# Residual input copied to the output in DRAM, results added there by accumulating DMAs, in a routed mixture-of-experts kernel

## The reference

```
xt   = x @ W.T + b + (x @ A[slot]) @ B[slot] * 2
gate = two experts of 16 for each token, with their scores
y    = sum over e of gate[:, e] * ((silu(xt @ w1[e] + b1[e]) * (xt @ w2[e] + b2[e])) @ w3[e] + b3[e])
z    = (silu(xt @ sw1 + sb1) * (xt @ sw2 + sb2)) @ sw3 + sb3
out  = x + y + z
```

## Time and profile before

| | |
|---|---|
| time, median of 3 runs | 166.63 us (165.42 to 168.01) |
| time of the profiled execution | 166.47 us |
| its span | 164.7 us |
| TensorE busy | 149.6 us (91%) |
| VectorE busy | 99.8 us (61%) |
| ScalarE busy | 52.9 us (32%) |
| GpSimd busy | 50.6 us (31%) |
| first gather issued | 72.51 us |
| first matmul of the tail | 145.53 us |
| last VectorE instruction starts | 161.57 us |
| TensorE clock granted | 1.000 over the whole span |

### The profile page before, as it was taken

The page is one execution under the profiler, slowest core; times in us unless marked ns, Lnnn a source line. Parts: engine busy times, 40 slices in busy tenths (PEclk is TensorE's granted clock), DMA queues, the critical chain, the costliest instruction groups (busy, mean ns, idle before and its releaser), DMA issues.

```text
span 164.7 us, 2590 instructions
## 1 busy us (share of the span) xinstructions
PE 149.6 (91%) x748; PEld 114.2 (69%) x749; DVE 99.8 (61%) x252; ACT 52.9 (32%) x110; POOL 50.6 (31%) x66
## 2 busy tenths in 40 slices
PE   3999999999979999997989989999999567789991
PEld 3777687887867777885867767778678355458770
DVE  2673495378967679978517873443453324358993
ACT  4542242623722161154363324324334122300000
POOL 6820240000000020436204675656656615230000
PEclk9999999999999999999999999999999999999999
DMA  5899938999965599998301467778777992336965
GB/s 170 291 359 333 412 153 247 398 423 416 400 204 211 158 374 391 384 452 284 117 13 44 153 180 228 225 271 246 222 273 236 323 401 91 115 127 223 352 256 194
DMA packets 16509, 42.62 MB, mean 259 GB/s; under 512 B 2192, under 2 KB 2192, under 8 KB 16240
## 3 DMA queue, kind: packets, MB, share of 16 engines
q1 hardware_dynamic: 11392, 25.41, 43.3%
q0 software_dynamic: 3616, 12.06, 21.7%
q10 hardware_dynamic: 1488, 4.98, 7.9%
HBM read 33.53 MB, written 8.91 MB: 258 GB/s over the span
## 4 chain that ended last, share of the span: by engine, by line
PE 69%; DVE 11%; DMA 11%; issue 4%; ACT 2%; POOL 1%; DVEq 0%; SPq 0%
PE bank L961 29%; PE bank L1133 16%; DMA xg_sb<-xt_rows,slot_tok 8%; PE bank L1151 7%; PE bank L1123 5%; DVE x_sb L911 3%; DVE x_sb L924 3%; PE bank L1021 2%; DMA xT_raw<-in_xT 2%; PE bank L1001 2%; DVE x_sb L919 2%; PE bank L1011 2%; PE bank L1032 1%; PE bank L1144 1%; PE bank L1113 1%
## 5 line engine op out<-in xcount | busy, mean ns | idle before, releaser
L1133 PE MATMUL bank<-w_sb,xgT_sb 128*128 x144 | 37.0, 382 | 1.5 <-issue 1.5
L1133 PEld LDWEIGHTS bank<-w_sb,xgT_sb 128*128 128x128 f32 x144 | 25.6, 190 | 12.5 <-issue 9.9
L451 POOL DMA_INDIRECT y_rows<-y_sb,slot_row x18 | 18.6, 1034 | 28.3 <-DVE y_sb L868 28.3
L856 DVE TENSOR_TENSOR pre_sb<-bank,b_sb 128x256 f32<-128x256 f32 x18 | 7.6, 425 | 28.2 <-PE bank L1133 21.8
L445 POOL DMA_INDIRECT xg_sb<-xt_rows,slot_tok x20 | 19.4, 971 | 11.9 <-issue 5.5
L1151 PE MATMUL bank<-w_sb,hT_sb 128*128 x36 | 18.6, 597 | 0.5 <-ACT hT_sb L594 0.5
L1123 PE MATMUL bank<-ident,xg_sb 128*128 128x128 f32 x72 | 10.9, 274 | 3.9 <-DMA xg_sb<-xt_rows,slot_tok 3.9
L961 PE MATMUL bank<-condW_h,xT_h 128*128 128x512 f32 x32 | 14.1, 441 | 0.3 <-DVE xT_l L662 0.3
L586 ACT COPY xgT_sb<-bank 128x512 f32<-128x512 f32 x18 | 10.5, 585 | 10.3 <-PE bank L1123 6.2
L961 PE MATMUL bank<-xtT_h,sw_h 128*128 128x512 f32 x32 | 13.2, 413 | 0.0
L868 DVE COPY y_sb<-bank 128x512 f32<-128x512 f32 x18 | 12.3, 684 | 1.5 <-PE bank L1151 1.5
(11 more groups left out here) (177 smaller groups left out, 277.2 us busy)
## 6 DMA issues: line engine op xcount, KB each, us to landing
w_sb<-in_w SPq DMA_DIRECT2D x8, 1024.0 KB, 9.3
w_sb<-in_w ACTq DMA_DIRECT2D x2, 2048.0 KB, 15.5
xt_rows<-xt_ring SPq DMA_DIRECT2D x8, 256.0 KB, 4.0
b_sb<-in_b SPq DMA_DIRECT2D x1, 2048.0 KB
x_sb<-in_x SPq DMA_DIRECT2D x8, 256.0 KB
low_sb<-y_rows SPq DMA_DIRECT2D x4, 512.0 KB
high_sb<-y_rows SPq DMA_DIRECT2D x4, 512.0 KB, 5.3
out<-x_sb SPq DMA_DIRECT2D x8, 256.0 KB, 2.7
```

The costliest lines, as they stand in the source:

```text
L451: pool.indirect_dma_start(y_rows, bass.IndirectOffsetOnAxis(ap=slot_row[:, b:b + 1], axis=0), y_sb[:, b % 2, :], None).then_inc(y_scattere ...
L856: dve.tensor_tensor(pre_sb[:, s % 2, :], bank[2 + s % 2][:, 0:2 * INTER], b12_sb[:, bass.ds(e * (2 * INTER), 2 * INTER)], ALU.add).then_in ...
L1133: mm = pe.matmul(bank[2 + s % 2][:, 0:2 * INTER], xgT_sb[:, s % 2, k, :], w12_sb[:, bass.ds(e * W12 + k * 2 * INTER, 2 * INTER)], start=(k ...
```

## The change

- SP no longer loads `x` into SBUF. It copies each tile of `x` to the same rows of `out`, DRAM to DRAM, at the same points of `y_copied`.
- The tiles are finished in `acc` (the place of `x_sb`). `add_low(i)` writes `low * val + shared`, `add_high(i)` adds `high * val`: two VectorE instructions per tile, in place of three for tiles 0 to 4 and two for tiles 5 to 7. The diagonal matmuls go.
- GpSimd adds each finished tile to `out` in DRAM by a DMA with `accum_op=ALU.add`; SP's stores go.
- `y_sb` becomes a ring of four (`y_place`). The waits for scatters count four semaphores, and eight registers hold the counts; VectorE's short instructions that compute them are fewer (11 go, 6 come).
- Gathers run six blocks ahead of the scatters instead of four (`AHEAD`). The ring `xg_sb` stays at four, so that a gather still waits for the transposes of the block four before it.
- TensorE loads `top` after block 0 and `left` after block 1, in place of after block 3 and after the loop, and no longer loads `first`. VectorE and ScalarE load `left` earlier too, VectorE also `first`.
- VectorE's part of the shared matrices is spread over blocks 0 to 6, which are written out up to 7.
- Of the last hidden product of the shared expert, three of four steps instead of two come before `turn_xg(0)`.

```diff
-LOW_ON_PE = (5, 6, 7)
 UNROLL = 4
+AHEAD = UNROLL + 2
+Y_RING = UNROLL
...
-        x_sb = at(112, "x_sb", [P, TILES, DIM])
+        acc = at(112, "acc", [P, TILES, DIM])
...
-        y_sb = at(132, "y_sb", [P, 2, DIM])
+        y_ring = at(132, "y_ring01", [P, 2, DIM]), at(176, "y_ring23", [P, 2, DIM])
...
+        def stored(eng, at, least):
+            return [eng.value_load(eid[0:1, at + s:at + s + 1], min_val=16 * least // Y_RING,
+                                   max_val=16 * -(-BLOCKS // Y_RING)) for s in range(Y_RING)]
...
-        def drained(eng, drain):
-
-            left = blocks_left(eng)
+        def drained(eng, left, drain):
+
...
-            sp.wait_ge(sh_up_done, 2 * IC)
             for i in range(TILES):
                 sp.wait_ge(y_copied, UNROLL + i)
-                sp.dma_start(x_sb[:, i, :], x[i * P:(i + 1) * P, :]).then_inc(x_in, 16)
+                sp.dma_start(out[i * P:(i + 1) * P, :], x[i * P:(i + 1) * P, :]).then_inc(x_in, 16)
...
+            low_counts = stored(sp, LOW_STORED_AT, LOW_BLOCKS)
+            counts = stored(sp, STORED_AT, FULL)
+            for s in range(Y_RING):
+                sp.wait_ge(y_scattered[s], low_counts[s])
+                sp.sem_inc(low_stored, 1)
+            sp.wait_ge(low_stored, Y_RING)
...
-            for n in range(TILES):
-                sp.wait_ge(acc_done, n + 1)
-                sp.dma_start(out[n * P:(n + 1) * P, :], x_sb[:, n, :]).then_inc(out_stored, 16)
             sp.wait_ge(out_stored, 16 * TILES)
...
             def group(g):
                 for b in range(g * UNROLL, (g + 1) * UNROLL):
-                    gather(b + UNROLL)
+                    if b + AHEAD < BPAD:
+                        gather(b + AHEAD)
                     scatter(b)
 
-            for b in range(UNROLL):
+            for b in range(AHEAD):
                 gather(b)
...
+            pool.wait_ge(x_in, 16 * TILES)
+            for i in range(TILES):
+                pool.wait_ge(acc_done, i + 1)
+                pool.dma_start(out[i * P:(i + 1) * P, :], acc[:, i, :], accum_op=ALU.add).then_inc(out_stored, 16)
...
-            for n, i in enumerate(LOW_ON_PE):
-                act.activation(diag[:, n, :], ident[:], ACT.Copy, scale=val[:, 0, i:i + 1]).then_inc(diag_ready, 1)
...
+            def add_low(i):
                 dve.wait_ge(shared_done, i + 1)
+                dve.scalar_tensor_tensor(out=acc[:, i, :], in0=low_tiles(first, i), scalar=val[:, 0, i:i + 1],
+                                         in1=shared_bank(i)[:], op0=ALU.mult, op1=ALU.add).then_inc(acc_shared, 1)
...
+            def add_high(i):
                 dve.wait_ge(high_in[i // 2], 16)
+                dve.wait_ge(acc_shared, i + 1)
+                dve.scalar_tensor_tensor(out=acc[:, i, :], in0=high_sb[:, i, :], scalar=val[:, 1, i:i + 1],
+                                         in1=acc[:, i, :], op0=ALU.mult, op1=ALU.add).then_inc(acc_done, 1)
+
             dve.wait_ge(low_in, 16 * TILES // 2)
+            for i in range(TILES):
+                add_low(i)
+                if i >= 3:
+                    add_high(i - 3)
+            for i in range(TILES - 3, TILES):
+                add_high(i)
...
-            shared_up(3, (1,), 0, KC // 2)
+            shared_up(3, (1,), 0, KC - 1)
...
             turn_xg(0, 0)
-            shared_up(3, (1,), KC // 2, KC)
+            shared_up(3, (1,), KC - 1, KC)
...
             for b in range(UNROLL):
                 steps(b, b)
-            top = last_group(pe)
+                if b == 0:
+                    top = last_group(pe)
+                if b == 1:
+                    left = blocks_left(pe)
...
-            first = low_at(pe)
...
-                if i in LOW_ON_PE:
-                    n = LOW_ON_PE.index(i)
-                    pe.wait_ge(diag_ready, n + 1)
-                    pe.wait_ge(low_in, 16 * TILES // 2)
-                    mm = pe.matmul(shared_bank(i)[:], diag[:, n, :], low_tiles(first, i), start=False, stop=True)
```

More of the change, by code:

```diff
@@ L45 @@
 DRAINED = BLOCKS - LOOP_END
-LOOP_AT, LEFT_AT, EVEN_AT, ODD_AT, LOW_EVEN_AT, LOW_ODD_AT, LOW_AT = range(BPAD, BPAD + 7)
+Y_RING = UNROLL
+LOOP_AT, LEFT_AT, LOW_AT = range(BPAD, BPAD + 3)
+STORED_AT, LOW_STORED_AT = BPAD + 4, BPAD + 4 + Y_RING
 LOW_BLOCKS = (K * T - T) // P
@@ L242, in program @@
         h_turned, hT_copied, y_done, y_copied = sem("h_turned"), sem("hT_copied"), sem("y_done"), sem("y_copied")
-        y_scattered = [sem(f"y_scattered{s}") for s in range(2)]
+        y_scattered = [sem(f"y_scattered{s}") for s in range(Y_RING)]
         shared_done, acc_shared = sem("shared_done"), sem("acc_shared")
-        diag_ready = sem("diag_ready")
         low_in = sem("low_in")
@@ L368, in _ @@
                              ).then_inc(low_in, 16)
[L369 to L373, removed]
+            for s in range(Y_RING):
+                sp.wait_ge(y_scattered[s], counts[s])
+                sp.sem_inc(rows_stored, 1)
+            sp.wait_ge(rows_stored, Y_RING)
             for n in range(TILES // 2):
                 sp.dma_start(high_sb[:, 2 * n:2 * n + 2], by_tile[1][:, 2 * n:2 * n + 2]).then_inc(high_in[n], 16)
-            for n in range(TILES):
-                sp.wait_ge(acc_done, n + 1)
-                sp.dma_start(out[n * P:(n + 1) * P, :], x_sb[:, n, :]).then_inc(out_stored, 16)
             sp.wait_ge(out_stored, 16 * TILES)
@@ L610, in _ @@
             top = last_group(act)
+            left = blocks_left(act)
             def group(b):
@@ L624, in _ @@
             each_group(act, 0, top, group)
-            drained(act, drain)
-            for n, i in enumerate(LOW_ON_PE):
-                act.activation(diag[:, n, :], ident[:], ACT.Copy, scale=val[:, 0, i:i + 1]).then_inc(diag_ready, 1)
+            drained(act, left, drain)
         @block.vector
@@ L828, in _ @@
             then(dve.tensor_tensor(slot_row[:], slot_f32, slot_empty, ALU.add))
[L830 to L835, removed]
+            dve.engine_nop().then_inc(slot_row_ready, 1)
+            then(dve.tensor_scalar(slots_back[:], cols[0:1, 0:Y_RING], -1.0, float(Y_RING - 1), ALU.mult, ALU.add))
+            then(dve.tensor_scalar(nused_f[:], ends[0:1, E - 1:E], 1.0 / P, None, ALU.mult))
             then(dve.tensor_scalar(low_base[:], padded[0:1, :], 0, None, ALU.is_gt))
@@ L864, in copy_y @@
                 dve.wait_ge(y_done, b + 1)
-                if not (isinstance(b, int) and b < 2):
-                    dve.wait_ge(y_scattered[s % 2], (b - s % 2) * 8)
-                dve.tensor_copy(y_sb[:, s % 2, :], bank[5 + s % 2][:]).then_inc(y_copied, 1)
+                if not (isinstance(b, int) and b < Y_RING):
+                    dve.wait_ge(y_scattered[s % Y_RING], (b - s % Y_RING) * (16 // Y_RING))
+                dve.tensor_copy(y_place(s), bank[5 + s % 2][:]).then_inc(y_copied, 1)
@@ L870, in _, with rest_hs @@
             add_bias(0, 0)
             times_up(0, 0)
[L872 to L878, removed]
+            def rest_hs(u):
+                dve.wait_ge(hs_hi, u + 1)
+                n, c = u // IC, u % IC
                 unit = (slice(None), c, slice(n * HALF, (n + 1) * HALF))
                 rest(hsT_split[1][unit], hsT_sb[unit], hsT_split[0][unit], hs_done)
[L881 to L887, removed]
@@ L888, in _, with rest_sw3, rest_b3s @@
-            top = last_group(dve)
+            def rest_sw3(c):
+                dve.wait_ge(sw3_hi, 1)
+                rest(sw3_split[1][:, c, :], sw3_raw[:, c, :], sw3_split[0][:, c, :], sw3_done)
+            def rest_b3s():
+                dve.wait_ge(b3s_hi, 1)
+                dve.tensor_tensor(b3s_split[32:64, :], b3s_raw[32:64, :], b3s_split[32:64, :].bitcast(F32), ALU.subtract
+                                  ).then_inc(b3s_done, 1)
+            for b in range(2 * UNROLL):
+                s = b % UNROLL
+                add_bias(b + 1, s + 1)
+                times_up(b + 1, s + 1)
+                copy_y(b, s)
+                if b < 4:
+                    rest_hs(b)
+                elif b < 6:
+                    rest_sw3(b - 4)
+                elif b == 6:
+                    rest_b3s()
+                if b == 4:
+                    top = last_group(dve)
+                if b == 5:
+                    left = blocks_left(dve)
+                if b == 6:
+                    first = low_at(dve)
@@ L901, in drain @@
                     copy_y(top + (UNROLL + s), s)
[L903 to L909, removed]
+            each_group(dve, 2 * UNROLL, top, group)
+            drained(dve, left, drain)
+            def add_low(i):
                 dve.wait_ge(shared_done, i + 1)
[L911 to L922, removed]
-                dve.wait_ge(high_in[i // 2], 16)
[L924 to L929, removed]
@@ L931, in _ @@
-            first = low_at(dve)
-            dve.wait_ge(low_in, 16 * TILES // 2)
[L933 to L949, removed]
@@ L1198, in _ @@
             each_group(pe, UNROLL, top, group)
-            drained(pe, drain)
```

(1 more changed line is left out.)

47 lines of the change are left out of this document (15 added, 32 removed).

## The result

| | before | after |
|---|---|---|
| time, median | 167.32 us (165.42 to 170.61, 4 runs) | 169.06 us (168.56 to 169.72, 4 runs) |
| profiled execution, time and span | 166.47 and 164.7 us | 168.87 and 167.1 us |
| start of the tail (first shared matmul) | 145.53 | 140.19 |
| end of VectorE | 162.26 | 157.0 |

The changed kernel takes 1.0174 of the time of the kernel before, 95% interval 1.0106 to 1.0242: slower, by 1 to 2.4%, where 165.2 us and a range of 162.0 to 168.6 were forecast. Some executions of a kernel are slower as a whole; the medians and ranges here hold them, the ratios leave them out. The table shows where the time went. The tail starts 5.3 us earlier and VectorE ends 5.3 us earlier, and yet the span is 2.4 us longer. All of the loss lies behind VectorE's last instruction.

A forecast was written before the change was run, and what follows sets the result against it. TensorE carries 69% of the chain, so its stalls and the tail count. Tail start 145.53 - 0.7 - 3.05 - 1.1 = 140.7, plus 22.7 of tail is 163.4 of span, plus 1.77 outside: 165.2 us, range 162.0 to 168.6.

The forecast's parts named there:

- part 6: Tail's end: GpSimd's accumulating stores finish at +22.7 us after the tail's start, making the tail 3.5 us longer.
- Part 1: Start of the blocks: three matmuls moved ahead of TensorE's 0.85 us wait for the first gather gain 0.7 us.
- Part 2: In the blocks: gathers issued earlier remove TensorE's stall for the gather of block 16, gain 3.05 us.
- The ring of four: Blocks, rows to scatter: four places in `y_sb` were said to remove no wait seen in the trace.
- Part 3: TensorE's register loads at loop entry, loop exit and ahead of the tail: gain 1.1 us, bounds 0 to 2.15.
- Part 4: Copies of x from DRAM to DRAM: cost 0, up to 3 us if they press on gathers.
- Part 5: VectorE in the tail: sixteen additions instead of 21 gain nothing, the last ending 17.15 us after the tail's start.
- Part 6, pitch 1.26: GpSimd's last four stores follow one another at 1.26 us, as its indirect DMAs do; bounds 0.33 and 1.26.
- Rival B: Tail's stores: a plain DMA costs GpSimd only 0.33 us, last issue at +17.45, time 163.6 us; chance 0.23.
- Part 6, the read, 0.9: Tail's stores: reading `out` before the addition writes it adds 0.9 us to the landing; bounds 0 and 3.6.
- The way of a plain one: Tail's stores: 2.8 us from a DMA's issue to its landing without the read, taken from the last scatter.
- rival D: Tail's accumulating DMAs don't overlap, each reading and writing back before the next; 173.6 us at 2.8 us each; chance 0.10.

The follow-up runs named there:

- e1: Changed kernel with plain stores by GpSimd in place of the accumulating ones, input left out of the sum: 164.34 us, 0.9843 of the kernel before.
- e2: Changed kernel with plain stores of `acc` by SP in place of GpSimd's accumulating ones, input left out of the sum: 161.58 us, 0.9685 of the kernel before.
- e4: Kernel before with one edit, gathers six blocks ahead: 165.87 us, 0.9949 of the kernel before.
- e6: e3 with TensorE loading `top` after block 3 and `left` after the loop, as before: 163.74 us, 0.9842 of the kernel before.
- e3: Changed kernel with the old tail (x in SBUF, old additions, diagonal matmuls, stores by SP): 161.89 us, 0.9709 of the kernel before.
- e8: Changed kernel with plain stores by GpSimd for tiles 0 to 6, accumulating for tile 7 alone, input left out of tiles 0 to 6: one run of 164.70 us.
- e10: e2 with tile 7 stored by GpSimd instead of SP, plain, input left out of the sum: one run of 163.78 us.
- e5: Kernel before with the new tail alone (x copied to `out` in DRAM, sixteen additions, accumulating DMAs by GpSimd): 174.21 us, 1.0487 of the kernel before.
- e9: Changed kernel, but tiles 4 to 7 with x in SBUF, three additions each and stores by SP: 164.06 us, 0.9854 of the kernel before.

## Why the prediction was wrong

The head and VectorE's tail went as forecast; the step that failed is part 6, "The stores by GpSimd": its 3.7 us from the last issue to the landing, of which 0.9 for the addition in DRAM, and its end of the program at that landing. The runs show 7.4 us, of which 4.6 for the addition (e1), and 2.0 more for GpSimd's drain (e2). Forecast and measured, as a sum of the span: 163.4; -0.5 for a tail that starts at 140.2 instead of 140.7; -1.9 for the last issue, at +17.1 instead of +18.97 after the tail's start; +3.7 for its landing, 7.4 us instead of 3.7; +2.4 for the time from that landing to the end, which the forecast had at nothing. That gives 167.1, the span measured. Of the 2.4, 0.4 lie behind the last landing in the kernel before too; the prediction took the span's end, 164.7, for that landing, which was at 164.3.

- **Part 1, 0.7:** 0.66 (the wait of 0.85 is now 0.19). Right.
- **Part 2, 3.05:** the stall is gone, so the size is right. But its reason was half of the truth. "The ring of four takes away no wait that the trace shows" was true and misleading: that wait was hidden behind the other one, and e4 uncovered it. Without the ring, which the forecast priced at nothing, the early gathers bring the tail forward by 2.3 us instead of 3.05, and are worth 1.1 us of span.
- **Part 3, 1.1:** the three gaps of 2.15 us became 0.41, a gain of 1.7, within the bounds. e6 puts 1.0 us on the two moved loads; e3 shows 0.54 for a tail that loads `first`.
- **Part 4, 0:** right. The copies DRAM to DRAM held nothing up, and e2, which has them, is as fast as e3, which hasn't.
- **Part 5, VectorE ends at +17.15:** 157.0 less 140.2 is +16.8, since the last four additions follow at 0.66 and not at the 0.75 that each takes. Fewer additions gained nothing, as forecast.
- **Part 6, pitch 1.26:** GpSimd's stores follow each other at 0.66, which is VectorE's pace, and it is the same for plain ones in e1; its own pitch is at most that. Here the Trainium skill (DMA: Bandwidth & Descriptors, anatomy of a DMA by the gpsimd path), which calls building descriptors a small part, was nearer than my row of indirect DMAs: GpSimd kept up with VectorE. Rival B had this term nearly right: the last issue at +17.1, for its 17.45.
- **Part 6, the read, 0.9:** measured by e1 against the changed kernel, the addition costs 4.6 us (164.7 less 160.1). The way of a plain one was right: 2.7 in e1, for 2.8. My bounds were those of a single DMA's way. What it costs is rate: full engines at less than half of the usual GB/s, by estimate 1.5 us for each 256 KB (256 KB by 170 GB/s), with eight issued in 7.6 us while the high rows were still coming. It comes near rival D's outcome by another mechanism: from the first issue, at 149.7, to the last landing, 164.7, it is 15 us for eight, 1.9 each, and I had put the point from which nothing is left of the gain at 1.9. I gave D 0.10, "each reads and writes back before the next is served". Had each only waited for another's answer, the engines should have stood partly idle; their share was 0.97 to 1.13 from 152 to 164, and 0.97 for the single one of e8.
- **Not in the forecast:** the drain, which ends 1.9 to 2.2 us behind the last landing where GpSimd issued the last transfer (the changed kernel, e1, e8, e10), and costs nothing where SP did (e2). What it waits for isn't shown.

What the chip gives for the parts of the change: head alone 0.971 (e3), tail alone 1.049 (e5), both 1.017.

## What to carry to other kernels

Price a DMA that adds in its target by the load on the DMA engines, here two to three times that of a plain one, and not only by its way; behind a tail in which the engines are already full it was not hidden here, and it held up plain stores too (e9). Let another engine than GpSimd issue the last store of a program: that was worth 2.0 us of span (e1 against e2). And when a wait is removed, look for the next wait on the same congested transfer: gathers in and rows out needed each its own slack before the stall was gone.

## What the runs showed of the hardware that was not expected

- GpSimd's closing drain ended 1.9 to 2.2 us after the landing of its last DMA in four kernels: the changed one (164.7 to 166.9), e1 (160.1 to 162.3), e8 (160.5 to 162.7) and e10 (159.9 to 161.8).
- Accumulating DMAs from SBUF to DRAM ran at 159 to 175 GB/s with all engines full (158 to 164 in the changed kernel); gathers, scatters and loads reached 365 to 389 in the earlier trace rows, and plain stores come to 367 for a full share in e1. GpSimd's own time for issuing one was 0.86 us and up, for a plain one 0.54 and up, for an indirect one 0.95 and up.
- The granted clock fell inside the work in two of the profiles, in the first microseconds of the tail: to 0.54 in e4, where TensorE had stood 1.27 us at the loop's end and 1.42 for `h_sb`, and to 0.62 in e6, where it had stood 1.45 us at the loop's end. The longest gap doesn't decide it: the kernel before stood 3.05 us in one piece at 1.00. Nor does the kernel: of its own 13 runs beside e6, the four with a mean clock of 1.000 took 165.51 to 166.92 us, the nine with 0.979 to 0.990 took 167.77 to 170.42. What makes the clock fall stays open.
